# Last stage of a fused transformer kernel: four experts over all tokens replaced by tiles of tokens sorted by expert

## The reference

```python
def moe(x, gate_w, gate_b, W1, b1, W2, b2):
    logits = x @ gate_w.T + gate_b
    top = jnp.argmax(logits, axis=-1)
    onehot = jax.nn.one_hot(top, N_EXPERTS, dtype=x.dtype)
    h = jax.nn.relu(jnp.einsum('btd,ehd->bteh', x, W1) + b1)
    y = jnp.einsum('bteh,edh->bted', h, W2) + b2
    return jnp.einsum('bted,bte->btd', y, onehot)
x = x + mla_attention(rmsnorm(x, norm1_w), ...)
x = x + moe(rmsnorm(x, norm2_w), gate_w, gate_b, W1, b1, W2, b2)
return x          # both lines start from the layer-normalised x; the result is added to x
```

## Time and profile before

| | |
|---|---|
| Three timed runs | 1390.89 us median (1388.12 to 1391.46) |
| The profiled execution | 1391.13 us, of which the span from first to last instruction is 1389.1 us |
| Busy in the span | PE 1217.6 us (88%), DVE 940.6 (68%), ACT 588.4 (42%), POOL 289.8 (21%) |
| Mean granted TensorE clock | 0.928 of full speed |
| The chain that ended last, in its largest lines | L1954 7%, L1932 7%, L703 4% of the span |

### The profile page before, as it was taken

The page is one execution under the profiler, slowest core; times in us unless marked ns, Lnnn a source line. Parts: engine busy times, 40 slices in busy tenths (PEclk is TensorE's granted clock), DMA queues, the critical chain, the costliest instruction groups (busy, mean ns, idle before and its releaser), DMA issues. The chain is left out here.

```text
span 1389.1 us, 36629 instructions
## 1 busy us (share of the span) xinstructions
PE 1217.6 (88%) x13743; PEld 832.4 (60%) x13751; DVE 940.6 (68%) x2794; ACT 588.4 (42%) x1311; POOL 289.8 (21%) x799
## 2 busy tenths in 40 slices
PE   3999998837958997988798997889999969999998
PEld 2888876725536774444576885458888634444443
DVE  4678839986365775999776885756777545555554
ACT  2688855651234663222343554844444411111111
POOL 1122220220311331000121221434555400000000
PEclk9999998967976998999898998879999969999999
DMA  9500000000000003000000000020000000000000
GB/s 288 152 4 3 3 3 1 2 1 1 2 1 2 3 3 122 1 1 1 1 1 2 3 3 2 1 62 3 3 3 3 2 1 8 8 8 8 8 8 15
DMA packets 26948, 25.84 MB, mean 19 GB/s; under 512 B 5664, under 2 KB 22816, under 8 KB 26528
## 3 DMA queue, kind: packets, MB, share of 16 engines
q1 hardware_dynamic: 25776, 23.43, 5.6%
q10 hardware_dynamic: 1008, 0.16, 0.1%
HBM read 21.49 MB, written 2.10 MB: 17 GB/s over the span
## 5 line engine op out<-in xcount | busy, mean ns | idle before, releaser
L671 PE MATMUL ps<-qTm,kT 32*128 32x512 f32 (+1 forms) x1024 | 251.5, 555 | 2.0 <-ACT probs L574 1.6
L703 PE MATMUL ps<-kT,qTm 32*128 32x128 f32 x3200 | 251.6, 292 | 0.8 <-DVE kT L408 0.8
L703 PEld LDWEIGHTS ps<-kT,qTm 32*128 32x128 f32 x3200 | 227.7, 203 | 6.1 <-issue 3.4
L1954 PE MATMUL ps<-kv_all,ctx_all 128*128 128x512 f32 x256 | 134.1, 605 | 5.2 <-DVE kv_all L1867 5.2
L1891 ACT ACTIVATE kv_all<-ps,b_col 128x512 f32<-128x512 f32 x64 | 44.0, 687 | 215.9 <-PE ps L1932 215.9
L1932 PE MATMUL ps<-q_all,ctx_all 128*128 128x512 f32 x256 | 132.3, 600 | 0.0
L380 DVE TENSOR_REDUCE neg_max<-ps 128x8 f32<-128x1024 f32 x72 | 87.9, 1221 | 59.8 <-PE ps L703 59.7
L1867 DVE TENSOR_SCALAR kv_all<-ps,b_col 128x512 f32<-128x512 f32 x64 | 48.0, 750 | 116.4 <-PE ps L1932 116.4
L574 ACT ACTIVATE probs<-ps 128x1024 f32<-128x1024 f32 x72 | 73.8, 1024 | 120.0 <-PE ps L713 120.0
L860 PE MATMUL ps<-probs,v_wide 128*32 128x128 f32 x3200 | 117.2, 280 | 4.9 <-DVE o_sb L429 1.7
L499 POOL CAST nm<-neg_max 128x16 bf16<-128x16 f32 (+1 forms) x132 | 27.0, 204 | 425.0 <-DVE neg_max L367 157.0
(11 more groups left out here) (375 smaller groups left out, 2601.3 us busy)
## 6 DMA issues: line engine op xcount, KB each, us to landing
ctx_all<-in_ctx SPq DMA_DIRECT2D x4, 1024.0 KB, 10.5
ctx_all<-in_ctxT SPq DMA_DIRECT2D x2, 2048.0 KB, 10.7
x_all<-in_x SPq DMA_DIRECT2D x4, 512.0 KB, 6.9
out<-x_all SPq DMA_DIRECT2D x8, 256.0 KB, 2.3
ctx_all<-in_W1T SPq DMA_DIRECT2D x1, 1024.0 KB, 5.2
tap_w<-in_conv_wT SPq DMA_DIRECT2D x1, 768.0 KB, 6.9
w_l<-in_w SPq DMA_DIRECT2D x2, 256.0 KB, 2.9
above<-in_c_above SPq DMA_DIRECT2D x1, 256.0 KB, 3.4
```

The lines of the kernel that those rows point to most:

```text
L671: nc.tensor.matmul(ps[:, bank, at:at + N], kT[rows_of(g), k, :], qTm[rows_of(g), k, 0:N], start=True, stop=False, skip_group_check=True)
L703: last = nc.tensor.matmul(dst, qTm[rows_of(g), k, 128 * i:128 * i + 128], kT[rows_of(g), k, :], start=False, stop=True, skip_group_check=True)
L1954: nc.tensor.matmul(ps[:, 4 + e % 2, :], w_down[:, c, :], hid[:, c % 4, :], start=c % 4 == 0, stop=c % 4 == 3).then_inc(sem("mo_down"), 1)
```

## The change

Each token is sent through its own expert only.

- Gate logits come from earlier products: in the latent stage 4 gate columns are added to the product of 320 columns and to the output projection of attention L4, so that `rows[b]`, a row of 261 numbers per token, holds the stream z (128), 4 unscaled gate logits, the sum x + z (128, added by POOL as `join` in attention L4) and the token's row number.
- In the last stage DVE chooses the experts of 16 batch rows at once (`choose`), counts with three small products how many tokens of each expert stand ahead, and gives each token a place such that every expert starts on a tile of 128. There are two batches of 16 rows; each has 16 + 3 tiles, 38 in all.
- POOL scatters the rows to their places in a DRAM area with one indirect DMA per batch row (32). Places that no token takes were blanked earlier with a row number out of range. SP then loads the sorted tiles back, in five DMAs per batch.
- For each tile, ACT and DVE load the expert's number into a register and copy that expert's weights (644 and 512 columns) into a ring of two; PE turns the tile and does 4 + 4 matmuls of 128 x 128 x 128; the relus are shared as before; DVE adds the result to the tile's x + z, and POOL writes the 128 rows to their places in the output with one indirect DMA per tile (38).
- Several tensors move into shared areas (`late`, `late2`); `sel` and its constant go.

The diff, cut to its core (the removed expert functions stand above; `late`, `late2` and the moved tensors are left out):

```diff
+GATE, JOIN, ROW_NO, ROW = D, D + N_EXP3, D + N_EXP3 + D, D + N_EXP3 + D + 1
+BATCHES = ((0, 16), (16, 16))
+TILES3 = 38
...
+        return ps[:, 7, 0:GATE + N_EXP3] if L == "L4" else ps[:, 7, 0:128] if L in LOW else ps[:, 6, 384:512]
...
+                dst = rows[:, b, 0:GATE + N_EXP3] if L == "L4" else stream[:, b, :]
                 nc.vector.tensor_tensor(dst, dst, product_at(L), ALU.add).then_inc(sem("x_updated"), 1)
...
+            def join(b, k):
+                pool.wait_ge(*after("x_updated", b + 1))
+                nc.gpsimd.tensor_tensor(rows[:, b, JOIN:ROW_NO], x_all[:, b, :], z_all[:, b, :], ALU.add)
...
-                work += [(4, lambda b, k: cut(b, k, 1))]
+                work += [(4, lambda b, k: cut(b, k, 1)), (9, join)]
...
-            nc.scalar.activation(sel[:], sel_col[:].unsqueeze(2).broadcast_to([128, 16, 128]), ACT.Copy)
...
             def take_latent(b, k):
+                nc.scalar.activation(rows[:, b, GATE:JOIN], ps[:, 2 + k, 320:320 + N_EXP3], ACT.Copy,
+                                     scale=inv_ln[:, b:b + 1])
...
-                nc.tensor.matmul(ps[:, 2 + k, 0:320], rowT[:, k % 2, :], w_h1[:], start=True,
+                nc.tensor.matmul(ps[:, 2 + k, 0:320 + N_EXP3], rowT[:, k % 2, :], w_h1[:], start=True,
...
+        def choose(dve, i):
+            q(V.tensor_tensor(lg, rows[:, items, GATE:JOIN], inv_all[:, items].unsqueeze(2).broadcast_to(full), ALU.mult))
...
+            q(V.tensor_tensor_scan(run, ones[:, 0:m], chosen, 0.0, ALU.mult, ALU.add))
+            q(V.tensor_tensor(earlier, run, chosen, ALU.subtract))
+            dve.sem_inc(sem("mo_chosen"), 1)
+            dve.wait_ge(sem("mo_counted"), i + 1)
+            q(V.tensor_copy(before, ps[:, 6 + i, 64:68]))
...
+            q(V.tensor_copy(places(i), place_f))
+            dve.sem_inc(sem("mo_placed"), 1)
...
+            def take_down(g):
+                if g >= 2:
+                    dve.wait_ge(sem("mo_down"), g - 1)
+                e = next(expert_vector.table)
+                nc.vector.tensor_copy(down_ring[:, g % 2, :], w_down[:, bass.ds(e, 1), :].rearrange("p o n -> p (o n)")
+                                      ).then_inc(sem("mo_down_set"), 1)
+            def bias(g): ...      # DVE: x + z of the tile plus the expert's second bias, 128 columns
+            def relu(g): ...      # DVE: chunks 1 and 3, 128 columns each
+            def finish(g):
+                dve.wait_ge(sem("mo_down"), g + 1)
+                nc.vector.tensor_tensor(row, row, ps[:, 6 + g % 2, 0:128], ALU.add).then_inc(sem("mo_done"), 1)
+            def step(tiles):
+                if 1 in tiles:
+                    take_down(tiles[1])
+                    bias(tiles[1])
+                    relu(tiles[1])
+                if 2 in tiles:
+                    finish(tiles[2])
...
+                yield engine.value_load(experts_of(i)[0:1, t:t + 1], min_val=0, max_val=N_EXP3 - 1)
...
         def expert_scalar(act):
+            for b in range(B):
+                nc.scalar.activation(z_all[:, b, :], z_all[:, b, :], ACT.Copy, scale=inv_all[:, b:b + 1]
+                                     ).then_inc(sem("mo_normed"), 1)
+            def take_up(g):
+                e = next(expert_scalar.table)
+                nc.scalar.activation(up_ring[:, g % 2, :], w_up[:, bass.ds(e, 1), :].rearrange("p o n -> p (o n)"),
+                                     ACT.Copy).then_inc(sem("mo_up_set"), 1)
+            def step(tiles):
+                if 0 in tiles:
+                    take_row(tiles[0])
+                    take_up(tiles[0])
+                if 1 in tiles:
+                    relu(tiles[1])
...
         def expert_gpsimd(pool):
+            for i, (first, n) in enumerate(BATCHES):
+                pool.wait_ge(sem("mo_placed"), i + 1)
+                for b in range(first, first + n):
+                    pool.wait_ge(sem("mo_normed"), b + 1)
+                    nc.gpsimd.indirect_dma_start(
+                        sorted_rows[i], bass.IndirectOffsetOnAxis(ap=places(i)[:, b - first:b - first + 1], axis=0),
+                        rows[:, b, :], None, bounds_check=(n + N_EXP3 - 1) * 128 - 1, oob_is_err=False
+                    ).then_inc(sem("mo_sorted_%d" % i), 16)
+            for g in range(TILES3):
+                pool.wait_ge(sem("mo_done"), g + 1)
+                nc.gpsimd.indirect_dma_start(
+                    out_rows, bass.IndirectOffsetOnAxis(ap=row[:, ROW_NO:ROW].bitcast(I32), axis=0),
+                    row[:, JOIN:ROW_NO], None, bounds_check=B * S - 1, oob_is_err=False).then_inc(sem("mo_stored"), 16)
...
+            for i, at, n, (tile_loaded, before) in tile_loads():       # SP; 1, 2, 4, 8, 4 and 1, 2, 4, 6, 6 tiles
+                sp.wait_ge(sem("mo_sorted_%d" % i), 16 * BATCHES[i][1])
+                sp.dma_start(...)
...
         def expert_tensor(pe):
+            def step(tiles):
+                if 0 in tiles:
+                    turn(tiles[0])        # waits for the tile's load, one transpose
+                if 1 in tiles:
+                    up(tiles[1])          # waits for the row copy and ACT's weight copy, 4 matmuls
+                if 2 in tiles:
+                    down(tiles[2])        # waits for DVE's weight copy and all four relus, 4 matmuls
```

More of the change, by code:

```diff
@@ L143, in build, with room @@
         x_all = sb("x_all", [S, B, D])
-        ctx_all = sb("ctx_all", [S, B, C])
+        late = sb("late", [S, B * C + 4352])
+        late2 = sb("late2", [128, 2176])
+        ctx_all = late[:, 0:B * C].rearrange("p (b d) -> p b d", b=B)
+        def room(area, at, *shape):
+            n = int(np.prod(shape))
+            names = " ".join("abc"[:len(shape)])
+            sizes = dict(zip("abc", shape))
+            return area[:, at:at + n].rearrange("p (%s) -> p %s" % (names, names), **sizes)
         q_all = sb("q_all", [S, B, D])
@@ L882, in attention_tensor @@
             whole_steps(pe, count, TURN_LAG[post], step)
+        TAIL = B * C
         wc = sb("wc", [128, 128])
@@ L1686, in latent_gpsimd @@
             pads_gpsimd(pool, 16)
+            nc.gpsimd.tensor_copy(rows[:, :, ROW_NO].bitcast(I32), row_no[:])
             def query(b, k):
@@ L1784, in build @@
-        chosen = work_m[:, 4096:8192].rearrange("p (k e t) -> p k e t", k=2, e=4)
-        xm_T = q_all[:, 0:8, :].rearrange("p a b -> p (a b)").rearrange("p (k t) -> p k t", k=2)
[L1787 to L1792, removed]
-            body(GROUPS - 1, 1)
-        def is_last(i):
-            return isinstance(i, int) and i == GROUPS - 1
@@ L1885, in expert_scalar @@
-        def expert_scalar(act):
-            def group(i, k):
-                for c in range(0, CHUNKS, 2):
-                    act.wait_ge(sem("mo_hidden"), i * CHUNKS + (c + 1))
-                    if c >= 4 or not is_first(i):
-                        act.wait_ge(sem("mo_down"), i * CHUNKS + (c - 3))
-                    nc.scalar.activation(hid[:, c % 4, :], ps[:, c % 2, :], ACT.Relu,
-                                         bias=b1_col[:, c:c + 1]).then_inc(sem("mo_relu_even"), 1)
-            loop_groups(act, group)
@@ new lines, in tile_loads, with expert_tiles @@
+        def tile_loads():
+            sizes = ((1, 2, 4, 8, 4), (1, 2, 4, 6, 6))
+            taken = iter([("x_loaded_%d" % j, 16) for j in range(4)] + [("ctx_loaded_%d" % j, 16) for j in range(4)]
+                         + [("l0_weights", 32), ("ctxT_loaded", 32)])
+            for i in range(len(BATCHES)):
+                for j, n in enumerate(sizes[i]):
+                    yield i, sum(sizes[i][:j]), n, next(taken)
+        def expert_tiles(sp):
+            for i, at, n, (tile_loaded, before) in tile_loads():
+                sp.wait_ge(sem("mo_sorted_%d" % i), 16 * BATCHES[i][1])
+                g = FIRST_TILE[i] + at
+                area, spot = (q_flat, g) if g < 15 else (kv_flat, g - 15)
+                sp.dma_start(area[:, spot * ROW:(spot + n) * ROW].rearrange("p (t w) -> p t w", t=n),
+                             sorted_rows[i][128 * at:128 * (at + n), :].rearrange("(t p) w -> p t w", p=128)
+                             ).then_inc(sem(tile_loaded), 16)
@@ L2301, in constants @@
     up, none = np.arange(1, SLOTS + 1), np.full(SLOTS, -1)
-    sel = np.zeros((128, 16))
-    for i in range(16):
-        sel[3 * i:3 * i + 3, i] = sel[64 + 3 * i:64 + 3 * i + 3, i] = 1
     row = t % 32
@@ L2321, in constants @@
         "c_iota_pair": np.tile(np.concatenate([up, none, none, up]), (128, 1)).astype(f32),
-        "c_sel": sel.astype(f32),
+        "c_tile_no": np.tile(np.arange(32), (128, 1)).astype(f32),
+        "c_row_no": (t[:, None] + 128 * np.arange(B)[None, :]).astype(np.int32),
         "c_sel_rows": sel_rows.astype(f32),
```

418 lines of the change are left out of this document (222 added, 196 removed).

## The result

The changed kernel takes 1252.1 us (median of four runs, 1246.8 to 1253.5) against 1390.1 us beside it: a ratio of 0.9001, 95% interval 0.8971 to 0.9031. The forecast was 1268, the range 1232 to 1325. The time is inside the range and 16 us under the forecast.

The account below looks back on a forecast made before the run. PE bounds the last stage (expert products, 220 of 272 us); head, 38 steps and tail end at 1263.1 against 1388.6, 125.5 us less, minus 3 us in earlier stages: 1391.1 - 122.5 = 1268.6 us, range 1232 to 1325.

Parts of the forecast that it names:

- What bounds before: Last stage, about 1117 to 1389 us: bound by PE, through the two expert products L1932 and L1954.
- the products' 220 us: Last stage: 256 pairs of matmul records, 0.86 us apart, make 220 of its 272 us and go with the change.
- Head: Last stage before the loop: moments, choice, 16 scatters at 1.3 us, landing and first tile's load, from 1117.7 to 1152.3 us.
- Loop: Last stage's 38 tile steps: 2.72 us each, DVE 2.42 plus 0.3 for port exclusion, 103.4 us in all.
- The fourth rival: Loop: register load hidden, lock not met, PE bounds at 1.98 us a step, 28 us less, 1240; chance 0.08.
- The lock: Loop: POOL and DVE exclude each other at shared ports, 0.3 us a step; as rival 38 us more, 1306, chance 0.09.
- its rival (1315): Loop: PE stays at 1.2 GHz and bounds at 3.95 us a step, adding 47 us; chance 0.18.
- POOL's price: Scatters and write-backs: 70 indirect DMAs at 2.36 us each keep POOL busy to 1292 us, time 1300; chance 0.14.
- slower: Whole kernel: 70 indirect DMAs above 3.7 us each outlast today's stage; at 4 us, 1415; chance 0.06.
- Tail: After the loop: last write-back costs 1.3 us of POOL and 2.3 us to land, ending at 1263.1 us.
- Earlier stages: Before the last stage: 3 us lost, from the latent stage's longer start (1.5) and extra ACT operation (1.5).
- The sixth ACT operation: Latent stage's first loop: 0.2 us more per item on ACT, hidden at best, 3.2 us at worst, taken as 1.5.

Follow-up runs that it names:

- the run with ACT alone edited: Changed kernel with the next tile's expert read into a register right behind the weight copy, on ACT only: 1.90 us a step, 111.3 us from first scatter to end.

## Why the prediction was right, and where it was not

**What bounds before** and that the products' 220 us go: borne out by the sum, though no run tests it alone. From the first moment to the end the last stage went from 271.7 to 127.4 us; 6.7 of the 144 us gained are lost before it.

**The total.** The forecast is nearer than its parts: 23.4 us too much in the loop less 7.9 us too little in the earlier stages and the tail leave the 15.1 us. That cancelling is luck.

**Head.** Right, 35.0 against 34.6 us. Moments 2.7 us as forecast. The choice 6.2 us of DVE operations (6.5). Then 1.0 us, which the sum did not have, from the choice's last operation (ends at 1133.17) to the first scatter; in the loop 0.8 us stand between a tile's finish and its write-back. Scatters at 1.28 to 1.30 us each, where 1.3 was picked between 0.43 and 2.36: no row set it closer, so the fit of that term is luck. Landing 1.6 us (2.3), the first load 2.9 us (2.3).

**Loop.** The mis-sized term: 2.72 us a step forecast, 2.05 measured, 38 x 0.67 = 25 us. Three steps of its working failed. First, DVE's five operations and its load were added up end to end to 2.42 us, and DVE does not set the step: the run with ACT alone edited has DVE's ring unchanged at 1.90 us a step. The operations lie closer than their durations add up to, and of the load only a hole of 0.45 us shows (the row at 1235.18 below); the rest runs beside the finish behind which it was said to stand. Second, ACT's load was said to run beside the row copy; it starts when that is nearly over, and ACT's ring, at 0.53 us more than its four operations back to back (1.52 us), was the bound. Third, PE's 1.98, from the earlier trace rows, is 1.90. The fourth rival (PE bounds at 1.98, the load hidden, 1240) had the step nearly right with a reason that falls: the load was not hidden, and with it ACT's ring was 0.15 us longer than PE's.

**The lock.** 0.3 us a step was allowed for; the loop shows nearly nothing of it. POOL's indirect DMAs take 976 ns on average in the loop, no more than the scatters that run alone (0.97 to 0.98 us), and the weight copies a median of 427 ns. In the changed kernel the two mostly pass each other: the write-back starts 0.34 us behind the copy, when 0.09 us of that are left. In the run without load and with fewer products they meet at nearly every step. A step of each, and ahead of the changed kernel's a copy that met a write-back earlier in the loop:

```profile
1180.96 0.97 POOL L2009 DMA_INDIRECT out<-q_all  x1 [0.31 <-issue]
...
1181.48 0.71 DVE L1914 COPY probs<-late 128x512 f32 x1 [0.45 <-issue]
...
1235.18 0.43 DVE L1914 COPY probs<-late 128x512 f32 x1 [0.45 <-issue]
1235.52 0.97 POOL L2009 DMA_INDIRECT out<-kv_all  x1 [1.08 <-DVE kv_all L1936]
```

```profile
1205.82 0.42 DVE L1914 COPY probs<-late 128x512 f32<-128x512 f32 x1
1205.94 1.14 POOL L2009 DMA_INDIRECT out<-kv_all  x1 [0.30 <-DVE kv_all L1936]
```

In the last pair the indirect DMA takes 1.14 us, 0.17 longer. The Trainium skill, "SBUF — State Buffer", section "SBUF: two separate sides", has the one that starts later block fully until the other is done; 0.30 us of the copy were left, so 0.13 us of POOL's work went on beside it. The other meetings in these runs say the same: with 0.365 us left an indirect DMA took 1.21 us, with 0.24 left 1.08, so what is left less 0.13 us is lost. DVE loses too: the copy at 1181.48, which starts 0.52 us behind an indirect DMA, took 0.71 us in place of 0.43. So the lock is real, up to 0.28 us a meeting, and what the forecast had wrong is how often the two meet. The earlier trace rows was a poor measure: 0.75 us came from a POOL memset of 1.19 us, not from an indirect DMA.

**Rivals.** The clock did as argued against its rival (1315): 0.50 while PE rests, 1.00 from 1166 us on. POOL's price and "slower" fell with 1.28 us.

**Tail.** Missed by 4.5 us: the forecast let the write-back land and ended there, and did not count the 5.8 us of drain that the phase's end puts behind 70 indirect DMAs. The trace of before has no such drain to read.

**Earlier stages.** 3.3 us forecast, 6.7 in this profile. The longer start of the latent stage is right (1.55 us against 1.5). The sixth ACT operation was taken at 1.5 us between 0 and 3.2 and cost more than the upper end: with it alone taken off ACT, the stretch from the latent stage's first product to the reciprocal in the last stage's moments, 256.1 us before, is 257.9 us, and in the nine profiles that have it 261.4 to 263.0, so 3.6 to 5.1 us. The earlier trace rows shows PE and ACT both near full; the pitch, 0.66 us without the operation and 0.82 with it, says that 0.16 us count in every item (32 x 0.16 = 5.1). The size goes with where the clock rises: in this profile the latent loop takes 26.3 us and half clock lasts 30.7 us at the start of attention L4, in others 27.4 and 23.9 us. The join in attention L4 cost nothing that can be seen.

## What to carry to other kernels

Do not add up an engine's operations for a software-pipelined loop; make the ring of each engine (its operations back to back, plus what stands with nothing running behind it) and take the longest, and count records per us instead of trusting a busy share near one. Read a register ahead, behind a long operation of the same engine, not ahead of the operation that needs it. Indirect DMAs on POOL cost the same 1.28 us whether they move 512 or 1044 bytes a row, so a head made of them is shortened by a smaller first batch, sized so that its tiles last as long as the second batch's scatters; and a stage that issues many of them pays 0.08 us for each in the drain at its end, unless a drain stands earlier in POOL's idle time.

## What was not expected of the hardware

POOL's drain: 0.08 us for each indirect DMA since the last drain (0.95 us behind 11, 4.89 behind 59, 5.78 behind 70), and uncounted in the busy times. POOL and DVE stop each other for up to 0.28 us when a write-back and a weight copy overlap, and pass unharmed when the write-back starts 0.34 us behind the copy. PE shown busy for 99% of a stretch in which a quarter of its matmuls could be left out at no gain. A wait of 2.9 us on PE in the loop was followed by 3.4 us of half clock, and where the wait was taken away, the half clock went too.
